# Gated attention: order of the products around the values, and who does the token sums and the 32 x 32 blocks

## The reference, cut to what matters

```python
q_mean = q.mean(axis=1)
gate = _soma_gate(q_mean, ...)                 # sigmoid of the 32 best scores of a sequence, 0 for all the others
dots = jnp.einsum('bhid,bhjd->bhij', q, k) * SCALE
dots = dots * (gate[:, None, :, None] * gate[:, None, None, :])
attn = jax.nn.softmax(dots, axis=-1)
out = jnp.einsum('bhij,bhjd->bhid', attn, v)
out = out.transpose(0, 2, 1, 3).reshape(Bx, Nx, INNER)
return out @ w_out.T + b_out
```

## Time and profile before

| | us |
|---|---|
| median of 3 runs (671.64 to 676.05) | 673.86 |
| the profiled execution's own time | 673.91 |
| its span, first to last instruction | 672.2 |
| PE busy in it | 552.9 (82%) |
| DVE busy | 505.7 (75%) |
| ACT busy | 360.5 (54%) |
| POOL busy | 269.6 (40%) |

### The profile page before, as it was taken

How to read it: one execution, slowest core, us unless ns; L and a number is a source line. 1 busy time by engine, 2 the same in 40 slices (tenths; PEclk the granted TensorE clock), 3 DMA queues, 4 the chain that set the end, 5 groups by cost and what they waited for, 6 DMA issues and landing times. The chain is left out here.

```text
span 672.2 us, 11846 instructions
## 1 busy us (share of the span) xinstructions
PE 552.9 (82%) x3809; PEld 313.0 (47%) x3809; DVE 505.7 (75%) x2306; ACT 360.5 (54%) x738; POOL 269.6 (40%) x501
## 2 busy tenths in 40 slices
PE   1875567988867999777999999999999898999870
PEld 1875467986656666311233333333333455465330
DVE  6599999454383778788899999999998056379784
ACT  5841134610200567501588788788878765466762
POOL 2001007721002476700354454545455454366784
PEclk9986675557967789855599999999999898999996
DMA  8000000210000066310011111111210000000001
GB/s 316 2 1 1 0 1 32 78 42 8 1 1 1 10 200 203 118 59 7 0 43 52 40 31 36 37 32 38 58 39 1 7 1 1 2 0 16 33 16 62
DMA packets 18876, 27.33 MB, mean 41 GB/s; under 512 B 3230, under 2 KB 14126, under 8 KB 18638
## 3 DMA queue, kind: packets, MB, share of 16 engines
q1 hardware_dynamic: 18174, 24.34, 11.6%
q10 hardware_dynamic: 576, 2.10, 0.9%
q0 software_dynamic: 64, 0.13, 0.1%
HBM read 14.11 MB, written 12.45 MB: 40 GB/s over the span
## 5 line engine op out<-in xcount | busy, mean ns | idle before, releaser
L904 DVE CUSTOM_DVE_ANT_0 w_qkvT<-d_pS,w_qkvT 128x512 bf16<-128x512 f32 x480 | 203.9, 485 | 17.3 <-PE d_pS L895 12.5
L1576 ACT ACTIVATE d_P<-pT 128x768 f32<-128x768 f32 (+1 forms) x192 | 165.9, 882 | 63.7 <-PE pT L1602 62.2
L1456 POOL TENSOR_SCALAR_AFFINE_SELECT d_P<-d_P 128x256 f32<-128x256 f32 x256 | 102.7, 415 | 134.7 <-ACT d_P L1576 134.7
L895 PE MATMUL d_pS<-Ks,Qs 48*128 48x512 bf16 x480 | 98.0, 325 | 13.3 <-DVE hadamard L904 8.9
L1602 PE MATMUL d_pO<-d_P,V 128*32 128x512 f32 (+3 forms) x1024 | 99.3, 463 | 1.4 <-POOL d_P L1456 0.9
L1602 PE MATMUL pT<-Qs,Ks 51*128 51x512 bf16 (+3 forms) x512 | 72.6, 311 | 1.9 <-ACT d_mT L1546 1.9
L895 PEld LDWEIGHTS d_pS<-Ks,Qs 48*128 48x128 bf16 x480 | 32.2, 96 | 56.7 <-DVE hadamard L904 52.0
L1602 PEld LDWEIGHTS pT<-Qs,Ks 51*128 51x128 bf16 x512 | 20.7, 94 | 73.8 <-ACT d_P L1576 42.8
L904 DVE DVE_READ_ACCUMULATOR2_ANT hadamard<- 128x1 f32 x512 | 42.5, 83 | 0.0
L1602 PEld LDWEIGHTS d_pO<-d_P,V 128*32 128x32 f32 x1024 | 21.3, 110 | 32.5 <-issue 29.6
L446 POOL MEMSET a_expS<- 1x1024 f32 x4 | 3.8, 945 | 78.7 <-DVE a_q L257 78.7
(11 more groups left out here) (314 smaller groups left out, 1073.1 us busy)
## 6 DMA issues: line engine op xcount, KB each, us to landing
Qs<-q_stack SPq DMA_DIRECT2D x32, 192.0 KB, 3.0
q_stack<-Qp SPq DMA_DIRECT2D x8, 384.0 KB, 2.5
X<-in_x_dram ACTq DMA_DIRECT2D x4, 512.0 KB, 6.2
n_rows<-N SPq DMA_DIRECT2D x4, 512.0 KB, 2.8
q_stack<-Qp SPq DMA_DIRECT2D x8, 256.0 KB, 2.5
out_dram<-e_moe SPq DMA_DIRECT2D x8, 256.0 KB, 2.0
w_qkvT<-in_w_qkvT_dram SPq DMA_DIRECT2D x1, 1536.0 KB
Ks<-k_stack SPq DMA_DIRECT2D x32, 48.0 KB, 3.2
```

The costliest lines, as they stand in the source:

```text
L895: last = nc.tensor.matmul(dst[:, at:at + w], top.Qs[c][rows, h % 8, 128 * q:128 * q + 128], top.Ks[c][rows, h // 4 % 2, 0:w], start=True, ...
L904: last = nc.vector.tensor_tensor_reduce(out=junk[:, at:at + w], in0=src[:, at:at + w], in1=top.wide_mask[:, 512 - w:512], scale=1.0, scala ...
L1456: last = nc.gpsimd.affine_select(out=view, in_=view, compare_op=ALU.is_ge, fill=0.0, base=0, pattern=[[0, 2], [1, 128]], channel_multiplie ...
L1576: nc.scalar.activation(P[pair % 4][:, :, P_AT[unit]:P_AT[unit] + w], pT[(3 * pair + unit) % 2][:, :, 0:w], ACT.Exp, scale=float(HD4) ** -0 ...
```

## The change

It has four parts, all in one phase.

**Token sums.** POOL adds the four rows of each of the last four sequences in two steps (`pairs`, `quads`). PE makes 16 products for the first four sequences and one product each for the others. The 4 idle products are gone. POOL clears PT after it has issued the gather, not before the token sums.

The diff, with some context and the semaphores' list left out:

```diff
@@ -605,7 +605,10 @@
...
         mv_ = ph.sb("meanv", [128, HEADS // 2, 2 * B])
-        ya = ph.sb("ya", [B, D])
+        yy = ph.sb("yy", [B, 2, D])
+        pairs = ph.sb("pairs", [128, B // 2, 2, D])
+        quads = ph.sb("quads", [128, B // 2, D])
+        turned = [ph.sb(f"turned{Q}", [128, HEADS, TOP_K]) for Q in range(NQ)]
         dY = ph.sb("dY", [B, D])
...
@@ -632,14 +635,27 @@
...
                 nc.gpsimd.memset(one[:, :], 1.0).then_inc(sm["one"], 1)
-                for Q in range(NQ):
-                    nc.gpsimd.memset(PT[Q][:, :, :], 0.0).then_inc(sm["zeroed"], 1)
+                later = top.N3[:, TILES // 2:, :].rearrange("p (b r) d -> p b r d", r=R)
+                nc.gpsimd.tensor_tensor(pairs[:, :, :, :], later[:, :, 0:2, :], later[:, :, 2:4, :], ALU.add)\
+                    .then_inc(sm["pairs"], 1)
+                pool.wait_ge(sm["pairs"], 1)
+                nc.gpsimd.tensor_tensor(quads[:, :, :], pairs[:, :, 0, :], pairs[:, :, 1, :], ALU.add)\
+                    .then_inc(sm["quads"], 1)
                 pool.wait_ge(top.rows_stored, 16 * CHUNKS)
...
                         .then_inc(rows_in[Q], 16)
+                for Q in range(NQ):
+                    nc.gpsimd.memset(PT[Q][:, :, :], 0.0).then_inc(sm["zeroed"], 1)
+                pool.wait_ge(sm["yu_copy"], 1)
+                nc.gpsimd.tensor_tensor(yu[:, :], yy[:, 0, :], top.b_out[:, :], ALU.add).then_inc(sm["yu"], 1)
+                nc.gpsimd.tensor_tensor(dY[:, :], yy[:, 1, :], yy[:, 0, :], ALU.subtract).then_inc(sm["dy"], 1)
+                pool.wait_ge(sm["zeroed"], NQ)
+                for Q in range(NQ):
+                    pool.wait_ge(sm["turned"], Q + 1)
+                    nc.gpsimd.tensor_copy(PT[Q][96:128, :, 96:128], turned[Q][96:128, :, :]).then_inc(sm["blocks_p"], 1)
 
...
@@ -706,17 +722,7 @@
...
                 dve.wait_ge(sm["v_psum"], 1)
-                nc.vector.tensor_copy(V[:, :, :], P1[:, :, :].rearrange("p (Q a) n -> p Q (a n)", a=2))\
-                    .then_inc(sm["v_out"], 1)
-
-                dve.wait_ge(sm["c_psum"], 1)
-                nc.vector.tensor_copy(mv_[:, :, :], P0[:, 0, 0:128].rearrange("p (i c) -> p i c", i=HEADS // 2))\
-                    .then_inc(sm["c_out"], 1)
-                dve.wait_ge(sm["yuc_psum"], 1)
-                nc.vector.tensor_copy(ya[:, :], P0[0:B, 1, 0:D]).then_inc(sm["yu_copy"], 1)
-                dve.wait_ge(sm["yu_copy"], 1)
-                nc.vector.tensor_tensor(yu[:, :], ya[:, :], top.b_out[:, :], ALU.add).then_inc(sm["yu"], 1)
-                nc.vector.tensor_tensor(dY[:, :], P0[0:B, 1, D:2 * D], ya[:, :], ALU.subtract).then_inc(sm["dy"], 1)
+                nc.vector.tensor_copy(V[:, 0, :], P1[:, 0:2, :].rearrange("p a n -> p (a n)")).then_inc(sm["v_out"], 1)
                 for Q in range(NQ):
...
@@ -748,15 +754,13 @@
...
                     dve.wait_ge(sm["probs_n"], Q + 1)
+                    nc.vector.transpose(turned[Q][:, :, :], diag[Q][:, :, :]).then_inc(sm["turned"], 1)
                     dve.wait_ge(sm["zeroed"], NQ)
-                    for j in range(4):
-                        rows = slice(32 * j, 32 * j + 32)
-                        last = nc.vector.transpose(PT[Q][rows, :, rows], diag[Q][rows, :, :])
-                    last.then_inc(sm["blocks"], 1)
+                    dve.wait_ge(sm["turned"], Q + 1)
+                    nc.vector.tensor_copy(PT[Q][0:32, :, 0:32], turned[Q][0:32, :, :]).then_inc(sm["blocks_d"], 1)
                 for Q in range(NQ):
                     dve.wait_ge(sm["O_psum"], Q + 1)
-                    nc.vector.tensor_copy(OT[Q][:, :, :],
-                                          (P0, P1)[Q][:, 0:2, :].rearrange("p a (i t) -> p (a i) t", t=128))\
+                    nc.vector.tensor_copy(OT[Q][:, 0:HALF, :], (P0, P1)[Q][:, 0, :].rearrange("p (i t) -> p i t", t=128))\
                         .then_inc(sm["O_out"], 1)
...
@@ -770,6 +774,9 @@
...
                     .then_inc(sm["qk_out_a"], 1)
+                act.wait_ge(sm["v_psum"], 1)
+                nc.scalar.activation(V[:, 1, :], P1[:, 2:4, :].rearrange("p a n -> p (a n)"), ACT.Copy)\
+                    .then_inc(sm["v_out_a"], 1)
                 for Q in range(NQ):
...
@@ -777,11 +784,28 @@
...
                     last.then_inc(sm["diag_a"], 1)
+                act.wait_ge(sm["c_psum"], 1)
+                nc.scalar.activation(mv_[:, :, :], P0[:, 3, 0:128].rearrange("p (i c) -> p i c", i=HEADS // 2), ACT.Copy)\
+                    .then_inc(sm["c_out"], 1)
                 for Q in range(NQ):
...
                         .then_inc(sm["probs"], 1)
+                act.wait_ge(sm["yuc_psum"], 1)
+                nc.scalar.activation(yy[:, :, :], P0[0:B, 3, 256:512].rearrange("b (k d) -> b k d", k=2), ACT.Copy)\
+                    .then_inc(sm["yu_copy"], 1)
+                act.wait_ge(sm["zeroed"], NQ)
+                for Q in range(NQ):
+                    act.wait_ge(sm["turned"], Q + 1)
+                    for j in range(1, 3):
+                        rows = slice(32 * j, 32 * j + 32)
+                        last = nc.scalar.activation(PT[Q][rows, :, rows], turned[Q][rows, :, :], ACT.Copy)
+                    last.then_inc(sm["blocks_a"], 1)
+                for Q in range(NQ):
+                    act.wait_ge(sm["O_psum"], Q + 1)
+                    nc.scalar.activation(OT[Q][:, HALF:, :], (P0, P1)[Q][:, 1, :].rearrange("p (i t) -> p i t", t=128),
+                                         ACT.Copy).then_inc(sm["O_out_a"], 1)
 
...
@@ -799,11 +823,13 @@
...
                 pe.wait_ge(sm["one"], 1)
-                for b in range(B):
+                for b in range(B // 2):
                     for r in range(R):
-                        last = mm(P1[:, 1, b:b + 1], top.N3[:, R * b + r, :], one[:, 0:1], r == 0, r == R - 1)
+                        mm(P1[:, 1, b:b + 1], top.N3[:, R * b + r, :], one[:, 0:1], r == 0, r == R - 1)
+                pe.wait_ge(sm["quads"], 1)
+                for b in range(B // 2, B):
+                    last = mm(P1[:, 1, b:b + 1], quads[:, b - B // 2, :], one[:, 0:1])
                 last.then_inc(sm["total_psum"], 1)
-                keep_busy(P0[:, 3, :], 4)
                 pe.wait_ge(sm["wide_index"], 1)
...
@@ -836,35 +862,39 @@
...
                 last.then_inc(sm["v_psum"], 1)
-                pe.wait_ge(sm["qk_out_a"], 1)
+                for Q in range(NQ):
+                    if Q == 0:
+                        pe.wait_ge(sm["qk_out_a"], 1)
+                    else:
+                        pe.wait_ge(sm["v_out"], 1)
+                        pe.wait_ge(sm["v_out_a"], 1)
+                    dots = (P0, P1)[Q]
+                    for h in range(HEADS):
+                        rows = slice(DH * (h % 2), DH * (h % 2) + DH)
+
+                        at = place(h)
+                        last = mm(dots[:, at // 4, 128 * (at % 4):128 * (at % 4) + 128],
+                                  QK[rows, h // 2, 0, 128 * Q:128 * Q + 128], QK[rows, h // 2, 1, 128 * Q:128 * Q + 128])
+                    last.then_inc(sm["dots_psum"], 1)
+                pe.wait_ge(sm["diag_d"], 1)
+                pe.wait_ge(sm["diag_a"], 1)
                 for i in range(HEADS // 2):
                     w = 2 * HEADS * DH + 128 * i
-                    last = mm(P0[:, 0, 16 * i:16 * i + 16], top.w_qkvT[:, w:w + 128], means[:, :, :])
+                    last = mm(P0[:, 3, 16 * i:16 * i + 16], top.w_qkvT[:, w:w + 128], means[:, :, :])
                 last.then_inc(sm["c_psum"], 1)
...
                     for i in range(HEADS // 2):
-                        last = mm(P0[0:B, 1, D * k:D * k + D], mv_[:, i, B * k:B * k + B], top.w_outT[:, i, :],
+                        last = mm(P0[0:B, 3, 256 + D * k:256 + D * k + D], mv_[:, i, B * k:B * k + B], top.w_outT[:, i, :],
                                   i == 0, i == HEADS // 2 - 1)
                 last.then_inc(sm["yuc_psum"], 1)
-                for Q in range(NQ):
-                    if Q == 0:
-                        pe.wait_ge(sm["dy"], 1)
-                    else:
-                        pe.wait_ge(sm["v_out"], 1)
-                    dots = (P0, P1)[Q]
-                    for h in range(HEADS):
-                        rows = slice(DH * (h % 2), DH * (h % 2) + DH)
-
-                        at = place(h)
-                        last = mm(dots[:, at // 4, 128 * (at % 4):128 * (at % 4) + 128],
-                                  QK[rows, h // 2, 0, 128 * Q:128 * Q + 128], QK[rows, h // 2, 1, 128 * Q:128 * Q + 128])
-                    last.then_inc(sm["dots_psum"], 1)
                 pe.wait_ge(sm["diag_d"], NQ)
                 pe.wait_ge(sm["diag_a"], NQ)
-                keep_busy(P1[:, 3, :], 24)
-                for Q in range(NQ):
-                    pe.wait_ge(sm["blocks"], Q + 1)
+                keep_busy(P1[:, 3, :], 10)
+                for Q in range(NQ):
+                    pe.wait_ge(sm["blocks_d"], Q + 1)
```

(28 more changed lines are left out.)

8 lines of the change are left out of this document (added).

## The result

The changed kernel takes 657.32 us, median of 4 runs (656.36 to 658.03), where the kernel before takes 672.82 in the same runs (4 runs, 671.64 to 676.05). The ratio is 0.977, with a 95% interval of 0.975 to 0.980. The forecast was 657.0 in 653.5 to 661.5. The profiled execution took 657.55 us, with a span of 655.8: 16.4 us less than before. In the trace 15.5 us of that are gone when the next phase starts (193.01 instead of 208.47), and the other 0.9 goes in the next phase, of which no line was changed: the phase behind it starts 16.5 us earlier (279.09 instead of 295.55), and the kernel's last operation comes 16.4 us earlier.

A forecast was written before the change was run, and what follows sets the result against it. The prediction took the changed phase, 69.5 of 672.2 us and serial with the others, to be set by waits between PE and DVE and a falling clock. Gains 5.4 + 7.1 + 2.5 + 1.8 = 16.8 us gave 657.0, range 653.5 to 661.5.

The forecast's parts named there:

- Token sums, 5.4 us: Choice to q and k products: POOL's additions shorten PE's sums, so row numbers and all behind them come 5.4 us earlier.
- Rival A: Clock worse than taken, falling at output products or rising late before q and k: 1.8 to 3.5 us lost; chance 0.20.
- Order, 7.1 us: After v: dots start at once, ahead of the means' products, which the softmax wait covers; 7.1 us gained.
- Transposes, 2.5 us: Before output products: one 128-row transpose and copies by three engines replace four transposes per Q; 2.5 us gained.
- rival C: Before output products: a 128-row transpose costs four of 32 rows, turning +2.5 into -1.7 us, 661.3; chance 0.04.
- B: Before output products: GpSimd's copy of its block comes last, 1.4 us behind ACT's for Q = 1, 658.5; chance 0.08.
- Clock, 1.8 us: Output products: with PE waiting less the high clock holds, so Q = 1's take 1.85 instead of 3.68 us; 1.8 gained.
- Outputs, 0: After output products: halving the output copies between DVE and ACT gains nothing, as Q = 1's copy lies beside Q = 0's projections.
- Rival D: q and k products to projections: clock stays low, 24 us lost against 16.8 won, 681; chance 0.02.

## Why the prediction was right, point by point

The places and mechanisms were right but for the end of the first part. That the time was hit within 0.3 us (657.0 for 657.3) is in part luck: one term was 1.5 us too large, and 0.9 us came in the next phase, which the sum had left out.

*Token sums, 5.4 us.* Right up to the row numbers (149.47 forecast, 149.42 measured), with POOL's additions at 2.41 and 1.26 us (2.32 and 1.28 forecast) and done at 141.7. Wrong behind them: "the gather's product at 160.34 moves with it" held, but not that the q and k products follow. The step that failed: "PT's clearing moves behind the gather ... POOL has nothing else there" looked at POOL's list alone. Beside it stood DVE's `selT`, the memset held it for 4 us, and gq stands behind `selT`. This alone puts the q and k products at 10.25 us behind `wide_index` and takes the missing 1.4 us: they start there even in the execution whose gather's product took 1.17 us. The gather's product also ran at the lower clock for all of its time, 0.84 us more than in the profile before; but in the changed kernel that is hidden behind the memset, and it would show only with PT cleared early (9.65 us in one such execution, 8.48 in the other). It is a matter of the moment at which the clock rises: the product took 1.14 and 2.10 us in two executions of one kernel. Rival A had priced this late rise at 0.8. The term was 3.9 us, not 5.4.

The Trainium skill ("GPSIMD Engine Reference", "Key points"), which the prediction used against the 32-row copies, names DVE instructions in a two-port mode as contending with GpSimd. The trace agrees at a place where I had not looked for it: `selT`, with one input, takes 0.47 us for 512 columns where DVE's operations with two inputs take 0.69 for as many. By the Trainium skill ("VectorE: DVE Perf Modes", "The perf-mode tier table") an fp32 `tensor_scalar` within SBUF runs in the 2x mode, which needs both read ports. That `selT` ran in this mode is inferred from its rate.

*Order, 7.1 us.* Right: from the start of v to the dots it was 10.73 us and is 3.53, 7.2 less. V's halves were in SBUF before Q = 1's dots asked for them, and the means' products had ended at 178.37, 2.6 us ahead of the blocks.

*Transposes, 2.5 us.* Right: 18.02 us from dots to Q = 1's products before, 15.49 now, 2.53 less; one transpose of 128 rows costs as much as one of 32 (0.71), so rival C fell. ACT's copies end last, as worked out, and POOL's 0.37 us before them, so B fell. The pair that B's reasoning spoke of did not come up: beside GpSimd's copy ran DVE's own copy and its sum (0.67 us, as elsewhere), and the multiplication started after it.

*Clock, 1.8 us.* Right in size, 3.68 to 1.97, and in place. But the idle products, which the prediction counted as what keeps PE busy until 184.4, are not needed. What changed is how long PE waits: the means' products now fill a part of the wait ahead of Q = 0's output products, and the quicker transposes shorten the waits ahead of both. Undoing either part brought the low clock back. A single wait's length doesn't tell: the clock stayed through 2.88 us and fell behind 2.86 us where another of 1.70 had gone before it. What decides between such waits stays open.

*Outputs, 0.* Right.

*The sum.* 3.9 + 7.2 + 2.5 + 1.7 = 15.3, to the measured 15.5 in the phase. Undone one at a time, the first three parts cost 3.9, 6.8 and 4.2 us up to the next phase; the clock's term is in the last two. The other 0.9 us of the span came in the next phase, where the clock stood otherwise: the products (to c_PK and c_PQ) took 1.91 us each at the low clock before, near 278 us, and 1.05 and 1.13 at 1.00 now (the prediction left 3 us either way for that, at a chance of 0.03). Runs scatter by as much.

Rival D never showed: no traced kernel met the low clock all through the middle of the phase. The most that it cost one was 3.3 us, with the transposes undone (1.7 in q and k, 1.6 behind the dots).

## What to carry to other kernels

When work is moved on one engine, look at what the other engines run at its new time, not only at what is queued behind it: a memset on GpSimd, moved to a free spot, stretched a DVE operation that stands ahead of one on the path. Products off the path belong behind those that start a long chain on other engines, and the chain's wait then hides them. Idle products want a check like any others: 10 of them here did nothing, 10 others held back a product whose first rows were there, and in a third place they held up the barrier. And a kernel's time alone can mislead by a microsecond or two where other phases wander; distances inside the traces settled what the parts are worth.

## What the runs showed of the hardware that was not expected

- GpSimd's fp32 memset held up DVE's `selT`, a one-input fp32 `tensor_scalar` within SBUF, until it was done. The first `selT` took 4.55 us and the second 0.47. It began 0.7 us before the memset's recorded start (152.23 and 152.94) and ended after both memsets (156.50). In the kernel before, the gather's issuing ran beside `selT` in the same way without the memset, and both took 0.96 us; so the memset is the cause. GpSimd's spans are rough, so the moment at which it first held DVE isn't shown. DVE's maximum searches and replacements, 0.68 and 0.66 us, took the same beside memsets and beside GpSimd's two-input additions.
- Something like it shows between the two engines' copies of 32 x 512: where DVE started first its copy took 0.42 us and GpSimd's 0.84, and where GpSimd's came first they took 0.84 and 0.61.
- The granted clock at the q and k products depends on the execution: they took 7.17 us in most, and 8.60 and 8.86 in two whose code is the same up to there. This moves the time by 1.4 to 1.7 us without any edit that bears on it.
